# A gated adapter layer on four batches: the residual copied into PSUM by rows instead of transposed by TensorE, and VectorE's order rewritten

## The reference, cut to what is computed

```
Wd, bd, Wu, bu, g, b = the expert's rows of W_down, b_down, W_up, b_up, ln_w, ln_b
h = einsum('bsh,bhk->bsk', x, Wd) + bd      # 512 -> 256
h = gelu(h, approximate=False)
h = einsum('bsk,bkh->bsh', h, Wu) + bu      # 256 -> 512
h = x + h                                   # residual
mean, var over the 512 features
h = (h - mean) * rsqrt(var + 1e-5)
return h * g + b
```

## Time and profile before

| | |
|---|---|
| median of 3 runs | 68.2 us (68.15 to 68.63) |
| the profiled execution's own time | 67.71 us |
| its span, first to last instruction | 65.8 us |
| TensorE busy | 57.7 us, 88% of the span |
| VectorE busy | 49.6 us, 75% |
| GpSimd busy | 40.3 us, 61% |
| ScalarE busy | 34.8 us, 53% |
| DMA | 14.75 MB, 224 GB/s in the mean |
| mean granted TensorE clock | 0.991 of full speed |

### The profile page before, as it was taken

The page is one execution under the profiler, slowest core; times in us unless marked ns, Lnnn a source line. Parts: engine busy times, 40 slices in busy tenths (PEclk is TensorE's granted clock), DMA queues, the critical chain, the costliest instruction groups (busy, mean ns, idle before and its releaser), DMA issues. The chain is left out here.

```text
span 65.8 us, 975 instructions
## 1 busy us (share of the span) xinstructions
PE 57.7 (88%) x300; PEld 48.1 (73%) x300; DVE 49.6 (75%) x95; ACT 34.8 (53%) x51; POOL 40.3 (61%) x43
## 2 busy tenths in 40 slices
PE   0999999999999999999999999999999999990000
PEld 0999446898888888868888888888999898870000
DVE  0059912539999998969989894499999979999910
ACT  0700299987897559999940729991056204040000
POOL 4000070794999389999998999999199002327300
PEclk9999999999999999999999999999999999999996
DMA  0899897069999999999995074300000752400750
GB/s 0 319 329 309 309 351 289 10 173 420 274 354 416 423 411 339 414 415 411 413 426 217 17 306 179 157 10 0 0 0 0 319 214 105 159 0 0 258 194 26
DMA packets 4468, 14.75 MB, mean 224 GB/s; under 512 B 496, under 2 KB 496, under 8 KB 4464
## 3 DMA queue, kind: packets, MB, share of 16 engines
q1 hardware_dynamic: 4176, 13.65, 54.8%
q10 hardware_dynamic: 288, 1.05, 4.2%
HBM read 10.50 MB, written 4.19 MB: 223 GB/s over the span
## 5 line engine op out<-in xcount | busy, mean ns | idle before, releaser
L214 POOL TENSOR_TENSOR x_lo<-x_raw,x_hi 128x512 fp32r<-128x512 f32 x10 | 13.2, 1346 | 1.0 <-ACT x_hi L274 1.0
L535 PE MATMUL y_ps<-wu_hi,hid_hi 128*128 128x512 f32 x32 | 13.4, 418 | 0.0
L230 POOL TENSOR_TENSOR rstd<-var_eps,minus_half 128x2 f32<-128x2 f32 (+1 forms) x10 | 6.4, 639 | 10.5 <-DVE var_eps L373 10.5
L541 PE MATMUL y_ps<-wu_hi,hid_lo 128*128 128x512 f32 x32 | 12.7, 397 | 0.0
L537 PE MATMUL y_ps<-wu_lo,hid_hi 128*128 128x512 f32 x32 | 12.5, 392 | 0.0
L365 DVE BATCH_NORM_STATS2 stats<-y_ps 128x6 f32<-128x512 f32 x16 | 10.9, 691 | 2.1 <-PE y_ps L541 1.9
L225 POOL TENSOR_TENSOR wu_lo<-w_raw,wu_hi 128x512 fp32r<-128x512 f32 x8 | 10.4, 1321 | 2.1 <-ACT wu_hi L284 2.1
L382 DVE SCALAR_TENSOR_TENSOR y_ps<-y_ps,mean_var,ln_gb 128x512 f32<-128x512 f32 x16 | 11.5, 750 | 0.0
L392 DVE SCALAR_TENSOR_TENSOR result<-y_ps,rstd,ln_gb 128x512 f32<-128x512 f32 x15 | 10.8, 742 | 0.3
L292 ACT ACTIVATE x_res<-x_raw,w_raw 128x512 f32<-128x512 f32 x16 | 10.2, 711 | 0.0
L520 PE MATMUL y_ps<-ident,x_res 128*128 128x128 f32 x64 | 8.6, 272 | 0.0
(11 more groups left out here) (35 smaller groups left out, 87.4 us busy)
## 6 DMA issues: line engine op xcount, KB each, us to landing
x_raw<-x_cols SPq DMA_DIRECT2D x6, 512.0 KB, 7.7
out<-result SPq DMA_DIRECT2D x6, 512.0 KB, 3.0
w_raw<-weights SPq DMA_DIRECT2D x4, 512.0 KB, 7.4
ln_gb<-ln_rows SPq DMA_DIRECT2D x4, 512.0 KB, 12.5
w_raw<-weights SPq DMA_DIRECT2D x3, 516.0 KB, 8.8
x_raw<-x_cols ACTq DMA_DIRECT2D x2, 512.0 KB, 4.1
out<-result SPq DMA_DIRECT2D x4, 256.0 KB, 2.4
w_raw<-weights SPq DMA_DIRECT2D x1, 260.0 KB, 3.6
```

The lines of the kernel that those rows point to most:

```text
L214: nc.gpsimd.tensor_tensor(x_lo[:, b % 2, k, :], x_raw[:, b, k, :], x_hi[:, b % 2, k, :].bitcast(F32), ALU.subtract).then_inc(x_lo_done, 1)
L535: nc.tensor.matmul(y_ps[:, t, :], hid_hi[:, p, j, rows], wu_hi[:, p, j, :], start=False, stop=False, skip_group_check=True)
L541: last = nc.tensor.matmul(y_ps[:, t, :], hid_lo[:, p, j, rows], wu_hi[:, p, j, :], start=False, stop=(j == JT - 1), skip_group_check=True)
```

## The change

For batches 1 to 3 the residual no longer goes through `x_res` and TensorE. The input `x` is given to the kernel a second time, by rows (`x_rows`), and SyncE loads 1 MB of it per batch over the columns in `x_raw`, which by then are used up. ScalarE copies each token tile into PSUM (`copy_rows`), after VectorE's `finish` of the same tile of the batch before, and TensorE waits for the copy (`copied`). The up bias, which was added by ScalarE with the residual, now comes in by one more product of 512 columns per token tile: a picking matrix `pick_r` of six rows (high and low part of each of the three batches' biases) by `bias_parts`. GpSimd builds the matrix's start, ScalarE rounds it, and VectorE splits the biases. Batch 0 keeps its transposes. VectorE's order within a batch is changed, and GpSimd's place for the first `inverse_std` as well.

```diff
+            def load_rows(b):
+                if b == 1:
+                    sp.wait_ge(early_x_lo_done, KT)
+                    sp.wait_ge(hid_ps_done, 1)
+                    sp.wait_ge(x_res_done, KT)
+                else:
+                    sp.wait_ge(x_lo_done, KT * (b - 1) - HALF)
+                    if b == 2:
+                        sp.wait_ge(early_x_lo_done, EARLY)
+                sp.dma_start(rows_of(b), x_rows[b]).then_inc(rows_in[b], DMA)
...
                 load_wd(b)
                 load_wu(b)
+                if b == 1:
+                    for i in range(1, B):
+                        load_bias(i)
                 load_ln(b - 1)
+                if b < LAST:
+                    load_rows(b)
             load_ln(LAST)
-            for b in range(LAST):
+            store(0)
+            load_rows(LAST)
+            for b in range(1, LAST):
                 store(b)
...
                     if b:
                         lo_wd(b + 1, 0)
                     lo_x(b + 1, 2)
+                    if b:
+                        inverse_std(b, 0, 2)
                     lo_x(b + 1, 3)
                     if not b:
                         lo_wd(b + 1, 0)
+                        inverse_std(b, 0, 2)
                     lo_wd(b + 1, 1)
-                    inverse_std(b, 0, 2)
                     inverse_std(b, 2, TT)
...
+            def copy_rows(b, t):
+                act.wait_ge(rows_in[b], DMA)
+                act.wait_ge(norm_done, TT * (b - 1) + t + 1)
+                nc.scalar.activation(y_ps[:, t, :], rows_of(b)[:, t, :], ACT.Copy).then_inc(copied, 1)
...
                 hi_wu(b)
-                residual(b)
+                if b == 1:
+                    act.wait_ge(pick_done, 1)
+                    nc.scalar.activation(pick_r[:], pick[:], ACT.Copy).then_inc(pick_r_done, 1)
                 if b < LAST:
                     hi_x(b + 1, 0)
                     hi_wd(b + 1)
                     gelu(b, 0)
+                    copy_rows(b, 0)
+                    copy_rows(b, 1)
                     gelu(b, 1)
+                    copy_rows(b, 2)
                     hi_x(b + 1, 1)
+                    copy_rows(b, 3)
...
+            def split_bias():
+                dve.wait_ge(bias_in, COPIED * DMA)
+                nc.vector.tensor_copy(bias_hi[:], bias_raw[:]).then_inc(bias_hi_done, 1)
...
+                nc.vector.scalar_tensor_tensor(out=bias_parts[:], in0=bias_hi[:].bitcast(F32),
...
+                finish(b, 0)
+                finish(b, 1)
+                if b == 0:
+                    split_bias()
...
+                if b and j == 0:
+
+                    pe.wait_ge(copied, TT * (b - 1) + t + 1)
...
+                    nc.tensor.matmul(y_ps[:, t, :], pick_r[:, b - 1, :], bias_parts[:],
+                                     start=False, stop=False, skip_group_check=True)
...
-                for t, j in [(0, 0), (1, 0), (0, 1), (1, 1)]:
-                    up(b, t, j)
+                up(b, 0, 0)
+                up(b, 1, 0)
+                up(b, 0, 1, low=False)
+                up(b, 1, 1, low=False)
+                up_low(b, 0, 1)
+                up_low(b, 1, 1)
```

More of the change, by code:

```diff
@@ L23, in conditional_adapter_kernel @@
     ln_rows: bass.AP,
+    x_rows: bass.AP,
+    up_bias_rows: bass.AP,
     out: bass.AP,
@@ L42, in conditional_adapter_kernel @@
     LAST = B - 1
+    COPIED = LAST
+    BIAS_ROWS = 2 * COPIED
     with ExitStack() as ctx:
@@ L54, in conditional_adapter_kernel @@
         ln_gb = sb("ln_gb", [P, B, 2, H])
-        x_res = sb("x_res", [P, 2, KT, S])
+        x_res = sb("x_res", [P, KT, S])
+        bias_raw = sb("bias_raw", [BIAS_ROWS, H])
+        bias_hi = sb("bias_hi", [BIAS_ROWS, H], F32R)
+        bias_parts = sb("bias_parts", [BIAS_ROWS, H], F32R)
+        minus_if_low = sb("minus_if_low", [BIAS_ROWS, 1])
+        pick = sb("pick", [BIAS_ROWS, COPIED, P])
+        pick_r = sb("pick_r", [BIAS_ROWS, COPIED, P], F32R)
         x_hi = sb("x_hi", [P, 2, KT, S], F32R)
@@ L95, in conditional_adapter_kernel @@
         ln_in = [sem(f"ln_in{b}") for b in range(B)]
+        rows_in = [None] + [sem(f"rows_in{b}") for b in range(1, B)]
+        bias_in = sem("bias_in")
         stored = [[sem(f"stored{b}{c}") for c in range(2)] for b in range(LAST)]
@@ L330, in _ @@
                     gelu(b, 0)
+                    copy_rows(b, 0)
+                    copy_rows(b, 1)
                     gelu(b, 1)
+                    copy_rows(b, 2)
                     hi_x(b + 1, 1)
-            for half in range(2):
-                for j in range(JT):
-                    gelu_half(half, j)
+                    copy_rows(b, 3)
+            gelu_half(0, 0)
+            gelu_half(0, 1)
+            copy_rows(LAST, 0)
+            gelu_half(1, 0)
+            copy_rows(LAST, 1)
+            gelu_half(1, 1)
+            copy_rows(LAST, 2)
+            copy_rows(LAST, 3)
             act.wait_ge(rstd_done, TT * LAST + SHARED_T + 1)
@@ L402, in _ @@
             for b in range(LAST):
[L403 to L410, removed]
+                tile_stats(b, 0)
+                tile_stats(b, 1)
+                moments(b, 0)
+                moments(b, 1)
+                shift_var(b, 0, 2)
+                centre(b, 0)
+                centre(b, 1)
+                tile_stats(b, 2)
+                finish(b, 0)
+                finish(b, 1)
+                if b == 0:
+                    split_bias()
+                if b + 1 == LAST:
+                    lo_hidden_half(0, 0)
+                tile_stats(b, 3)
+                moments(b, 2)
+                moments(b, 3)
+                shift_var(b, 2, 4)
                 if b + 1 < LAST:
-                    finish(b, 0)
-                    finish(b, 1)
                     lo_hidden(b + 1, 0)
-                    finish(b, 2)
-                    finish(b, 3)
+                else:
+                    lo_hidden_half(0, 1)
+                centre(b, 2)
+                centre(b, 3)
+                finish(b, 2)
+                if b + 1 < LAST:
                     lo_hidden(b + 1, 1)
                 else:
[L419 to L423, removed]
                     lo_hidden_half(1, 0)
-                    finish(b, 3)
+                finish(b, 3)
             for t in range(TT):
@@ L513, in down_half, with place_residual, up @@
                 last.then_inc(hid_ps_done, 1)
[L515 to L518, removed]
+            def place_residual(t):
+                pe.wait_ge(x_res_done, KT)
                 for k in range(KT):
[L520 to L525, removed]
+                    nc.tensor.matmul(y_ps[:, t, k * P:(k + 1) * P], x_res[:, k, t * P:(t + 1) * P], ident[:],
+                                     start=(k == 0), stop=False, is_transpose=True, skip_group_check=True)
+            def up(b, t, j, low=True):
                 p = b % 2
@@ L538, in up, with up_low @@
                                  start=False, stop=False, skip_group_check=True)
+                if b and j == 0:
+                    if (b, t) == (1, 0):
+                        pe.wait_ge(pick_r_done, 1)
+                        pe.wait_ge(bias_parts_done, 1)
+                    nc.tensor.matmul(y_ps[:, t, :], pick_r[:, b - 1, :], bias_parts[:],
+                                     start=False, stop=False, skip_group_check=True)
+                if low:
+                    up_low(b, t, j)
+            def up_low(b, t, j):
+                p = b % 2
+                n = JT * b + j + 1
+                if b == LAST and t >= 2:
+                    n += JT
                 if t == 0 or (t == 2 and b == LAST):
                     pe.wait_ge(hid_lo_done, n)
-                last = nc.tensor.matmul(y_ps[:, t, :], hid_lo[:, p, j, rows], wu_hi[:, p, j, :],
+                last = nc.tensor.matmul(y_ps[:, t, :], hid_lo[:, p, j, t * P:(t + 1) * P], wu_hi[:, p, j, :],
                                         start=False, stop=(j == JT - 1), skip_group_check=True)
@@ L552, in _ @@
                 down(b, 1, b == 0)
-                for t in range(TT if b == 0 else 2):
-                    place_residual(b, t)
-                for t, j in [(0, 0), (1, 0), (0, 1), (1, 1)]:
-                    up(b, t, j)
+                if b == 0:
+                    for t in range(TT):
+                        place_residual(t)
+                up(b, 0, 0)
[4 more added lines that the diff above has]
+                up_low(b, 1, 1)
                 for t in range(2, TT):
-                    if b:
-                        place_residual(b, t)
                     for j in range(JT):
```

49 lines of the change are left out of this document (37 added, 12 removed).

## The result

The changed kernel takes 84.1 us (median of 4, 83.2 to 84.7) against 68.2 us: 1.227 times as long, 95% interval 1.217 to 1.238. The prediction had said slower, 72.9 us, 74.6 at most. The direction held; the forecast slowdown, 4.7 us, was three tenths of the 15.9 that came.

A forecast was written before the change was run, and what follows sets the result against it. TensorE was taken to bound the middle, VectorE's 9.8 us the end. VectorE's batch 3 start 4.5 us late plus 0.2 made 67.7 + 4.7 = 72.4 profiled, 72.9 in terms of the median; range 69.6 to 74.6.

The forecast's parts named there:

- the bias product, taken at 0.23 us: TensorE, batches 1 to 3: four six-row products a batch, 0.23 us each by their 512 columns, 0.92 a batch; ends 0 and 0.39.
- the clock: Rival: the 3.4 us first stall lowers TensorE's clock to 1.2 GHz, 1.8 to 3.6 us more, 75 us; chance 0.05.
- the chain: Late load, gelu, copies and late GpSimd low parts stall TensorE, so VectorE starts batch 3 at 57.4, 4.5 us late.
- gelu behind the rounding that waits for a load: ScalarE: batch 2's down weights land at 26.5, rounding ends at 27.5, batch 1's gelu parts at 28.1 and 28.7.
- the first hole released by a copy: TensorE, before batch 1's up product: idle 3.4 us from 25.93, until ScalarE's copy of tile 0 at 29.3.
- the low parts late by VectorE's order: Batch 0's variance at 25.5 instead of 23.1, so GpSimd's first `wu_lo` ends at 27.5; GpSimd's list is 2.3 us behind.
- a hole before batch 3's first up product: Third stall: TensorE needs `rstd` and two `wu_lo`, ending at 56.5; VectorE begins on the tile at 57.4, before 52.93.
- The stall within batch 3's first half slice: Second stall, 1.8 us: GpSimd's last `wd_lo` is ready at 50.25, TensorE wants it at 48.5.
- The two bias instructions of VectorE: Batch 0: 0.46 and 0.66 us, ends 0.2 and 1.6 together; nothing added for port waits, GpSimd being idle at 23.3 to 25.5.
- The gain of 2.5 us in the sum: TensorE: transposes of 1.74 us a batch replaced by bias products of 0.92, 0.82 gained, 2.5 in three batches; ends 5.2 and 0.5.
- the late load: SyncE's queue: 1 MB of rows, 2.5 us, ahead of batch 2's down weights, landing at 26.5 instead of 23.8; upper end 27.5.
- the step that called the bias issues hidden: SyncE: three bias issues of 0.5 us each, hidden by the weights' 8.8 us to land; 0.2 added for their packets.

The follow-up runs named there:

- The order alone: Kernel before with only the changed kernel's VectorE and GpSimd order, no row loads, copies or bias product: 70.9 us, 1.046 times before.
- 128 rows: Changed kernel with the picking matrix and biases filled up with zero rows to 128: 75.3 us.
- old order: Changed kernel with VectorE's and GpSimd's order of the kernel before: 78.9 us, 1.14 times before.
- kept busy: Changed kernel with 20 unused products ahead of batch 1's up product and 8 ahead of batch 3's: 77.1 us.
- both holes filled: Changed kernel with unused products in both TensorE pauses and the bias product of 128 rows: 74.6 us, 1.101 times before.
- three mends: Changed kernel with 128-row bias product, batch 1's gelus ahead of batch 2's roundings, and VectorE's and GpSimd's order of before: 69.2 us, 1.019 times before.
- gelus first: Changed kernel with batch 1's gelus and copies of tiles 0 and 1 ahead of ScalarE's roundings for batch 2: 78.2 us.

## Why the prediction was right and wrong

Two steps of the sum failed: the bias product, taken at 0.23 us, and the clock, for which nothing was added. Undone one after the other they lead back to within 1.7 us of the forecast: 84.1 us, 77.1 with the holes filled, 74.6 with products of 128 rows besides, where 72.9 had been forecast.

**Right: the chain.** The four things it named are there: gelu behind the rounding that waits for a load, the first hole released by a copy, the low parts late by VectorE's order, and a hole before batch 3's first up product (1.75 us, until 62.9). The order alone costs 2.7 us in the kernel before and 4.6 with the copies (and with the gelus first). The stall within batch 3's first half slice came only in the variants with 128 rows that kept the order (1.3 to 1.4 us); in the changed kernel TensorE was too late to meet it. The two bias instructions of VectorE took 0.40 and 0.74 us with GpSimd idle, so it was right to add no wait for them.

**Wrong: the bias product at 0.23 us, with 0.39 as the upper end.** It was taken by its columns, and the upper end from the busy time of a product whose neighbours have its shape. It costs 0.62, and 1.0 at half clock: the twelve are 7.4 us at full clock, more than the 5.2 of the transposes they replace. The gain of 2.5 us in the sum was a loss of 2.2. Busy time was no bound, since it does not contain a weight load that cannot be hidden. The Trainium skill's rule that was weighed ("TensorE: Matmul & The Clock Gate", "Step-by-step: what each phase is for") goes by the columns alone, and 6 against 128 rows of zeros contradict it: same columns, 4.1 us apart in twelve products.

**Wrong: the clock, a rival with 0.05.** It was argued away by the full clock up to 64.5 us in the trace of before, 5 us after the last product, and the sum holds nothing for it. The rows of after, clock in the last column but two:

```profile
28.00:29.00 1.00, 0.00 (x0) 0.00 (x0) 0.00 (x0) 0.74 (x1) 1.00 (x2) 1.00 1.09 356
29.00:29.50 0.50, 0.00 (x0) 0.00 (x0) 0.00 (x0) 0.50 (x2) 0.50 (x1) 0.91 0.88 336
29.50:30.00 0.50, 0.00 (x0) 0.00 (x0) 0.00 (x0) 0.50 (x2) 0.50 (x2) 0.50 1.08 426
...
39.00:39.50 0.50, 0.50 (x2) 0.17 (x1) 0.50 (x3) 0.00 (x0) 0.00 (x0) 0.50 0.98 401
39.50:40.00 0.50, 0.50 (x2) 0.22 (x2) 0.39 (x4) 0.00 (x0) 0.00 (x0) 0.85 1.05 426
```

It fell to 1.2 GHz at 29.4, some 3 us after the last product, and came back at 39.7, 8.6 us after TensorE had resumed. Filling the holes gave back 7.0 us. One trace's idle tail had been read as a licence for idle stretches in the middle, which it was not. The second fall, at 63.5, followed a hole of under 2 us. The rival's price (1.8 to 3.6 us, hence 75) was about right for one fall: the first covers 17 products, three of them bias products, which took 8.6 us where they take 5.1 at full clock, so 3.5. That there would be a second, over 8 more and 12 of half the length, some 2.5 us, it did not say.

**Mis-sized, in part by luck of the execution: the late load.** Predicted at 26.5, batch 2's down weights landed at 28.2. SyncE's and the DMA's rows:

```profile
13.55 2.36 SPq L199 DMA_DIRECT2D bias_raw<-up_bias_rows  x3
16.10 0.34 SPq L195 DMA_DIRECT2D ln_gb<-ln_rows  x1
...
18.19 0.41 SPq L189 DMA_DIRECT2D w_raw<-weights  x1
```

```profile
16.00:18.00 2.00, 2.00 (x11) 1.63 (x10) 1.97 (x3) 1.79 (x2) 2.00 (x3) 1.00 0.74 234
```

The three bias loads of 4 KB took 0.79 us each to issue, not 0.5, and the next load went out 2.5 us later than before (13.56), the weights' own 3.2 us later (18.19, before 15.03). The DMA engines were 0.74 busy at 16 to 18 us, so the step that called the bias issues hidden is doubtful; no run was made without them. The weights then took 10.1 us to land, before 8.8. In four variants with the same loads ahead of them (128 rows, old order, kept busy, both holes filled) they took 8.8 to 9.0 and landed at 26.6 to 27.0, close to the forecast, with the three mends 10.1 again: the further 1.2 us are not in every execution, and their cause is open. The first hole was 4.8 us instead of 3.4; in the two of the four that leave it open it was 2.65 and 3.5.

What the copies and the 3 MB more of loads cost by themselves was not tried alone; with three mends, they and TensorE's gain together come to between 0.3 us less and 2.9 more than before, which holds zero.

## What to carry to other kernels

Before a small matrix product replaces something larger, look at whether its shape equals its neighbours': a product of 6 rows between full ones cost 0.4 us more than the same columns with zero rows added, and one of 64 rows did no better. A kernel whose TensorE never pauses holds a full clock as hidden capital; price each new wait at its length plus the products that then run at half clock, and look at the mean clock of every execution, which is its sign (0.86 to 0.88 with both holes, 0.975 to 0.981 with both filled). The spread between executions alone is not: that of the changed kernel was 1.5 us, and the kernel before, without holes, once spread over 2.3 us (67.1 to 69.4). And moving a small instruction on which a third engine waits (here a variance of 0.17 us) moves that engine's whole list.

## What the runs showed of the hardware that was not expected

- A weight load of 6 or 64 rows isn't brought ahead of the running product, nor is the load behind it: 0.39 us for each pair at full clock, about 0.57 at half, though the load itself is as short (181 ns and 187 ns).
- How long the clock stayed at half after TensorE had resumed differed widely: 8.6 us after the first hole and 7.5 after the second (62.9 to 70.4), 16.8 with the old order and six rows, 3.2 with the product of 128 rows (one trace each).
- Nor did it fall after one idle time: 5.2 us after the last product in the kernel before, in the changed one 3.2 us in the first hole, 2.4 at the second (0.6 after TensorE had resumed) and 1.6 after its last product.
- Holes of 1.75 and 1.83 us left the clock full in one program's profiled execution (gelus first), while one of 1.75 us in the changed kernel was followed by a fall.
- Three DMAs of two rows each held SyncE for 2.36 us.
